# A fused attention and expert layer on one core: the expert weights' loads issued by SP from a row number in a register, with a new table of priorities

## What is computed

```python
xn = _layernorm(x, axis=-1)
x = x + _L0_attn_ref(xn, ...) + _L0_ffn_ref(xn, ...)
```

```python
topv, topi = jax.lax.top_k(gout, K)      # K = 2 of E = 8
z = (x @ W1 + b1) * (x @ W2 + b2)
g = z @ Wg + bg
y = (g * sigmoid(g) * (z @ Wl + bl)) @ W3 + b3
```

## Time and profile before

| what | value |
|---|---|
| median of 3 runs | 904.22 us (900.74 to 907.99) |
| the profiled execution, its own time | 901.63 us |
| its span | 899.9 us |
| PE busy | 662.3 us (74%) |
| DVE busy | 556.5 us (62%) |
| POOL busy | 508.1 us (56%) |
| ACT busy | 298.8 us (33%) |
| mean granted TensorE clock | 0.812 |

### The profile page before, as it was taken

The page is one execution under the profiler, slowest core; times in us unless marked ns, Lnnn a source line. Parts: engine busy times, 40 slices in busy tenths (PEclk is TensorE's granted clock), DMA queues, the critical chain, the costliest instruction groups (busy, mean ns, idle before and its releaser), DMA issues.

```text
span 899.9 us, 30793 instructions
## 1 busy us (share of the span) xinstructions
PE 662.3 (74%) x13276; PEld 506.4 (56%) x13276; DVE 556.5 (62%) x1233; ACT 298.8 (33%) x519; POOL 508.1 (56%) x565
## 2 busy tenths in 40 slices
PE   3345749788877896887796797778787887896741
PEld 2235737566656665665664565566565666674531
DVE  6899875548447747576538545774467665723651
ACT  2210043424335235243343343332434352313120
POOL 3722178848682864768724847756857654521311
PEclk9555569989789798888997898988969996878585
DMA  8212123232122131132221321422323302113341
GB/s 314 111 59 70 60 54 76 71 99 54 63 76 71 49 90 62 41 89 80 75 55 40 89 47 53 112 84 39 68 74 85 96 8 56 52 22 103 113 140 70
DMA packets 62950, 69.10 MB, mean 77 GB/s; under 512 B 40080, under 2 KB 45200, under 8 KB 62688
## 3 DMA queue, kind: packets, MB, share of 16 engines
q0 software_dynamic: 10672, 34.78, 13.6%
q1 hardware_dynamic: 51712, 30.42, 11.8%
q10 hardware_dynamic: 432, 1.94, 0.5%
HBM read 47.45 MB, written 19.66 MB: 75 GB/s over the span
## 4 chain that ended last, share of the span: by engine, by line
PE 27%; POOL 26%; issue 18%; DVE 17%; DMA 6%; ACT 4%; SPq 2%; POOLq 0%; DVEq 0%; ACTq 0%
POOL y_d L1034 6%; POOL xs L1009 4%; PE ps_shared L1614 4%; PE ps_g L1610 4%; POOL z L1068 3%; PE ps_x L1610 3%; DVE acc L1380 3%; POOL ssq_o L1060 3%; PE ps_shared L1752 2%; PE ps_l L1610 2%; PE ps_shared L1610 2%; DMA w_mid<-y_d 2%; POOL sumsq L974 2%; PE ps_shared L1619 1%; PE ps_shared L1668 1%
## 5 line engine op out<-in xcount | busy, mean ns | idle before, releaser
L1034 POOL DMA_INDIRECT y_d<-work,put_i x92 | 92.4, 1004 | 45.2 <-issue 26.5
L1009 POOL DMA_INDIRECT xs<-xn_d,owner_i x92 | 94.2, 1024 | 28.2 <-issue 26.3
L1610 PE MATMUL ps_g<-z,w_mid 128*128 128x512 f32 x276 | 87.7, 461 | 27.3 <-POOL z L1068 23.4
L1610 PE MATMUL ps_x<-xr,w_up 128*128 128x512 f32 x276 | 97.2, 468 | 12.3 <-issue 10.8
L1610 PEld LDWEIGHTS ps_g<-z,w_mid 128*128 128x128 f32 x276 | 58.1, 220 | 45.8 <-issue 33.4
L1380 DVE SCALAR_TENSOR_TENSOR acc<-pre,late_sb,acc 128x512 f32<-128x512 f32 x72 | 59.6, 828 | 39.0 <-ACT acc L1127 38.1
L1068 POOL TENSOR_TENSOR z<-work,z 128x512 fp32r<-128x512 f32 x46 | 59.8, 1299 | 39.1 <-ACT z L1234 38.7
L1610 PE MATMUL ps_l<-z,w_mid 128*128 128x512 f32 x276 | 79.1, 423 | 0.0
L1581 DVE SCALAR_TENSOR_TENSOR work<-ps_g,w_plain,work 128x512 f32<-128x512 f32 x46 | 34.3, 746 | 54.1 <-ACT work L1240 54.0
L1610 PEld LDWEIGHTS ps_x<-xr,w_up 128*128 128x128 f32 x276 | 53.7, 218 | 24.1 <-issue 11.5
L1240 ACT ACTIVATE work<-ps_g,w_plain 128x512 f32<-128x512 f32 x46 | 31.5, 685 | 103.0 <-PE ps_g L1610 103.0
(11 more groups left out here) (248 smaller groups left out, 1493.8 us busy)
## 6 DMA issues: line engine op xcount, KB each, us to landing
xa_d<-xr SPq DMA_DIRECT2D x8, 512.0 KB, 2.7
xa<-xa_d SPq DMA_DIRECT2D x8, 512.0 KB, 3.7
w_mid<-y_d SPq DMA_DIRECT2D x16, 256.0 KB, 3.4
system_d<-masked SPq DMA_DIRECT2D x8, 256.0 KB
x_res<-hidden SPq DMA_DIRECT2D x8, 256.0 KB, 2.8
part_d<-x_res SPq DMA_DIRECT2D x8, 256.0 KB
comb<-part_d SPq DMA_DIRECT2D x8, 256.0 KB, 2.8
out<-comb SPq DMA_DIRECT2D x8, 256.0 KB, 2.0
```

The source lines that it names most:

```text
L1009: pool.indirect_dma_start(xs[par][:, c, :], None, xn_d.rearrange("w p (c d) -> (w p c) d", c=CPW), bass.IndirectOffsetOnAxis(owner_i[:, w ...
L1034: pool.indirect_dma_start(y_d, bass.IndirectOffsetOnAxis(put_i[:, w * CPW + c:w * CPW + c + 1], 0), y_sb[par][:, c * D:(c + 1) * D], None) ...
L1610: made = pe.matmul(to, weights[a], x[b], start=start and n == 0, stop=stop and n == 2)
```

## The change

`load_split` and `load_plain` go from POOL's list to SP's. SP waits for the same semaphores as POOL did, reads the first row number of the tile from partition 0 of `row_i` into a register (`value_load`), and issues a plain transfer of 128 rows from there. The rows of one expert are neighbours in DRAM, so the same bytes are moved. The costs of the two steps in `FLOW` change with it, and the table of priorities `PULL` is a new one, with a second table `LEAN` beside it that was empty: a step's priority now also grows or falls with the number of its window or tile. Every engine's order is therefore another.

```diff
-    "load_split": [[(POOL_, 1.2, 7.0)]], "load_plain": [[(POOL_, 1.2, 5.0)]], ...
+    "load_split": [[(SP_, 1.2, 6.0)]], "load_plain": [[(SP_, 1.2, 4.0)]], ...
-PULL = {"beta_T": -100, "blend": 100, "choose": -200, "combine": -400, "conv": -150, "conv0": 150, "count": 300,
...
-LEAN = {}
+PULL = {"beta": -100, "blend": -50, "choose": 400, "conv": -350, "conv0": 450, "delta_T": 50, "delta_again": 400,
...
+LEAN = {"beta": -30, "beta_T": 15, "combine": 60, "delta_T": -35, "delta_again": -60, "down": 10.4, "fir": -5,
...
@@ block.sync @@
+                elif name == "load_split":
+                    sp.wait_ge(S["placed"], 1)
+                    if w:
+                        sp.wait_ge(S["up_low"], w)
+                        sp.wait_ge(S["mid_low"], w)
+                    row = sp.value_load(row_i[0:1, w:w + 1], min_val=0, max_val=(EXPERTS - 1) * P)
+                    sp.dma_start(w_split[:, :], expert_split[bass.ds(row, P), :]).then_inc(S["in_split"], 16)
+                elif name == "load_plain":
+                    if w < 2:
+                        sp.wait_ge(S["placed"], 1)
+                    else:
+                        sp.wait_ge(S["y_sb"], w - 1)
+                    row = sp.value_load(row_i[0:1, w:w + 1], min_val=0, max_val=(EXPERTS - 1) * P)
+                    sp.dma_start(w_plain[par][:, :], expert_plain[bass.ds(row, P), :]).then_inc(S[f"in_plain{par}"], 16)
@@ block.gpsimd @@
-                elif name == "load_split":
-                    pool.wait_ge(S["placed"], 1)
-                    if w:
-                        pool.wait_ge(S["up_low"], w)
-                        pool.wait_ge(S["mid_low"], w)
-                    pool.indirect_dma_start(w_split[:, :], None, expert_split,
-                                            bass.IndirectOffsetOnAxis(row_i[:, w:w + 1], 0)).then_inc(S["in_split"], 16)
-                elif name == "load_plain":
-                    if w < 2:
-                        pool.wait_ge(S["placed"], 1)
-                    else:
-                        pool.wait_ge(S["y_sb"], w - 1)
-                    pool.indirect_dma_start(w_plain[par][:, :], None, expert_plain,
-                                            bass.IndirectOffsetOnAxis(row_i[:, w:w + 1], 0)).then_inc(S[f"in_plain{par}"], 16)
```

More of the change, by code:

```diff
@@ L84 @@
     "choose": [[(DVE_, 5.0)], [(ACT_, 0.5)]], "count": [[(PE_, 1.2)]], "place": [[(DVE_, 9.0)]],
-    "load_split": [[(POOL_, 1.2, 7.0)]], "load_plain": [[(POOL_, 1.2, 5.0)]], "split_up": [[(ACT_, 0.65)], [(POOL_, 1.4)]], "split_mid": [[(ACT_, 1.1)], [(DVE_, 1.9)]],
+    "load_split": [[(SP_, 1.2, 6.0)]], "load_plain": [[(SP_, 1.2, 4.0)]], "split_up": [[(ACT_, 0.65)], [(POOL_, 1.4)]], "split_mid": [[(ACT_, 1.1)], [(DVE_, 1.9)]],
     "load_xs": [[(POOL_, 5.1, 7.6)]],
@@ L111 @@
 }
-PULL = {"beta_T": -100, "blend": 100, "choose": -200, "combine": -400, "conv": -150, "conv0": 150, "count": 300,
-        "delta_again": 350, "down": -300, "fetch": -100, "fir": 500, "fir_l": -400, "fir_l_T": -50, "fir_l_out": 150,
-        "fir_s_T": 200, "full": -100, "fuse": 300, "fuse2": 450, "gate_T": 50, "gates": 350, "gelu": 100, "hid": 100,
-        "inv": -400, "inverse_out": -50, "k_T": -50, "ln": -300, "load_plain": 200, "load_x": -50, "load_xs": -450,
-        "load_xt": 50, "masks": 350, "masks0": -600, "mid_g": 350, "mid_l": -250, "mix_s": -350, "mix_v": 300,
-        "norm": -300, "o": -200, "o_T_out": -100, "on_state": -250, "out": 600, "owned": 200, "place": 600, "q_T": -150,
-        "rank": -600, "rms": -350, "solve_mul": -500, "solve_sum": -100, "split": -50, "split_mid": 50,
-        "split_qkv": -50, "split_up": -50, "sumsq": -300, "swish": 500, "times": 300, "turn": 100, "u_adj": 500,
-        "up1": -300, "up2": 300, "v_T": 350, "v_act": -100, "v_again_T": -100, "v_b": -200, "w_T": -200, "w_T_out": 450,
-        "x_res": 300, "xn_out": 100, "y_out": -150, "z": 50, "zeros": -350}
@@ L122 @@
-LEAN = {}
+PULL = {"beta": -100, "blend": -50, "choose": 400, "conv": -350, "conv0": 450, "delta_T": 50, "delta_again": 400,
+        "diag": 150, "fir": -150, "fir_l": -600, "fir_l_T": 150, "fir_l_out": 150, "full": -100, "fuse": 250,
+        "fuse2": -50, "gate": -200, "gates": 500, "inv": 300, "inverse_out": -100, "ln": -50, "load_split": -400,
+        "load_x": -50, "load_xs": -600, "low": 300, "mark": 600, "masks": 250, "masks0": -300, "mid_g": 100,
+        "mid_l": -450, "mix_s": 250, "norm": -300, "normed": 50, "o": 600, "o_T_out": -150, "out": 50, "own": -100,
+        "owned": -150, "place": 500, "products": -200, "q_T": -150, "rank": -200, "rms": -350, "solve_sum": -100,
+        "split_mid": 450, "split_up": 200, "store": -400, "swish": 500, "turn": -50, "u_adj": -50, "up2": 600,
+        "v_T": -300, "v_again": -100, "v_again_T": 50, "v_b": -400, "w_T": 150, "w_T_out": 600, "x_res": -100,
+        "xn_out": -50, "y_out": 150, "y_put": -300, "z": -50, "zlow": -300}
@@ new lines @@
+LEAN = {"beta": -30, "beta_T": 15, "combine": 60, "delta_T": -35, "delta_again": -60, "down": 10.4, "fir": -5,
+        "fir_l_T": 30, "fir_l_out": -30, "full": 5, "fuse": -15, "fuse2": -5, "gate": 15, "gate_T": 5, "inv": -30,
+        "inverse_out": 10, "ln": -25, "load_split": -1.7, "load_xs": 5.2, "load_xt": -5, "mark": -30, "masks": 15,
+        "mid_l": 5.2, "mix_v": 30, "normed": 25, "o": -5, "o_T_out": -25, "owned": 30, "products": 30, "project": 5,
+        "rms": 10, "split": -1.3, "split_mid": 6.9, "split_up": -15.6, "state": 5, "store": 15, "sumsq": -15,
+        "times": 10.4, "u": 15, "u_out": 60, "v_T": 5, "v_act": 45, "v_again": -35, "v_again_T": -30, "v_b": -30,
+        "x_res": -5}
```

## The result

The changed kernel takes 909.77 us (median; 902.74 to 917.29), the kernel before 904.1 in the same series: ratio 1.0055, 95% interval 1.0032 to 1.0079. That is half a per cent slower, within the 1% that I had called no change; the forecast was 889 us. So of the 12.5 us between the two spans only 5.7 are the change's.

What follows compares the result with a forecast made beforehand. No engine was full; two interwoven streams of dependent steps bound the kernel, with POOL's time dearest. Terms -15 + 0 + 4 + 2 - 5 = -14 on the median 904.22 gave 890, stated as 889 us; range 868 to 913.

Steps and rivals of the forecast that it cites:

- POOL relief: Middle: 63 us leave POOL's list; at most 29 us come off the path, half taken, -15 us.
- the load's cost: Loads on SP: register read 1.2 us, landing 5 to 7 us as now, offset by less lateness; 0, ends at 5 us.
- SP in the way: SP's strict list: loads and the windows' system, solve and inverse steps queue behind each other; +4 us (0 to 30).
- start, from the loads: Start: three loads with register reads go out one after another, so DVE's `split_mid` waits; +2 us (0 to 3).
- the new order, tail: End: window 6's `fuse` products go ahead of the last `down`, removing waits for filter and gelu; -5 us (-10 to 0).
- Where I am least sure: All other instructions reordered: costs 0 if PE fills as well; one part in fifty per tile is 14 us either way.
- the whole of POOL's share comes off: POOL's full 29 us come off the path and the windows run earlier; 872 us, chance 0.17.
- the rival of SP as the knot: On SP, loads wait behind a solve or inverse not ready, and tiles wait for them; 928 us, chance 0.12.
- The one queue: On SP's queue, a solve or inverse read right behind a load waits for all of it; 904 us, chance 0.08.
- The signs that I had named: Right: POOL busy about 458 us, chain share near 22%; wrong: ACT's `w_split` waits over 60 us, PE's middle share not above 80%.

Runs made afterwards that it cites:

- series 5: Chip where the kernel before takes 905.73 us: old order with loads on SP 880.14 us (0.9710); changed kernel with both tables emptied 911.21 us (1.0075).
- series 2: Against the kernel before (996.74 us): changed kernel 0.9842; old order with loads on SP 0.9607; old order with nearly all weight loads left out 0.9576.
- series 3: Old order, loads on SP, POOL keeping the old loads' waits 0.9716, time 0.9673, both 0.9765; changed kernel with later `y_put` 0.9875; all against the kernel before.
- series 4: Old order, loads on SP, POOL's waits kept, plus spare transfers: large indirect 1.0014, small indirect 1.0047, plain 0.9772; changed kernel with `LEAN` emptied 1.0161.

## Why the prediction was wrong

The sum of the prediction, beside what the two traces of the 905 us kind and the old order with loads on SP give:

| term | forecast, us | measured, us | from |
|---|---|---|---|
| POOL relief, the load's cost, SP in the way (the middle) | -15 + 0 + 4 = -11 | -23.7 | 658.3 to 634.6 |
| start, from the loads | +2 | +0.6 | 151.8 to 152.4 |
| the new order, start | 0 | +3.7 | 152.4 to 156.1 |
| the new order, middle | 0, "14 us either direction" | +43.4 | 634.6 to 678.0 |
| the new order, tail | -5 | -13.0 | 91.3 to 78.3 |

The loads alone moved the tail by +1.5 (89.8 to 91.3). The old order with loads on SP was profiled in series 5, the other two before any series, so that a few us of each row can be the chip's. And the executions are not equally typical: that of the changed kernel lies 4.1 us above its median, that of before 2.5 below, that of the old order at it. So the order's rows sum to some 4 us too much. By the ratios, the same is 0.971 for the loads and 1.0055 / 0.971 = 1.036 for the order: about -26 and +32 us.

**The step that failed** is the one under "Where I am least sure": that an order of all other instructions "that fills it as well as now costs 0", with 14 us either way. It cost +34 us between the spans, +32 by the ratios. I had priced the moves that I looked at, the four loads at the start, window 3's inverse and the last tile, and let the rest cancel; nothing in the trace of before spoke for that, and a range of one part in fifty was too narrow for a list that is new from end to end. That 909.77 still lies inside my range of 8 in 10 (868 to 913) is luck: two misses of opposite sign met, the loads -26 where I had -9 and the order +32 where I had -5. What can be said of these 34.1 us: 12.2 are PE's busy time (655.8 to 668.0, at a granted clock of 0.86 instead of 0.89 in the middle), 21.9 its idle time. Between the cuts PE's busy time grows by 21.2; 9.9 of it is attention's work of the last stretch (46.23 to 36.29), which moved there. The tail's gain is in part only a move, and the middle pays for it. The idle time that nothing in the profile explains, summed over the groups of PE and PEld, is 270.7 us in the old order with loads on SP and 320.1 in the changed kernel (in PE's own rows, where no gap counts twice, 42.7 and 70.7). So the added idle time is of the kind that the profile puts down to no other engine. Why the new order has more of it, and which of its many swaps does it, no run told apart. The empty tables' 1.0075 suggests that the new tables as a whole hold no good order for these costs, rather than that one entry spoils it.

**The POOL relief** had the right sign and was too small. Taking half of 29 us was wrong for the size; the upper end, POOL's share of the chain (46%) times the 63 us that left it, was near what the loads alone gave (-26 us between medians). The rival "the whole of POOL's share comes off" forecast 872 for the sum with the tail's -5; without the order's part it would be 877, measured 880.14. Whether that nearness is the mechanism or luck stays open. The same rule fails on the slower chips. The kernel before, profiled again in series 2, has these busy times and this chain:

```profile
PE 718.2 (72%) x13276; PEld 538.3 (54%) x13276; DVE 563.3 (57%) x1233; ACT 299.6 (30%) x519; POOL 506.4 (51%) x565
...
PE 41%; issue 18%; DVE 15%; POOL 11%; DMA 6%; ACT 4%; another core or an unknown queue 2%; SPq 2%; DVEq 0%; POOLq 0%; ACTq 0%
```

By the rule, POOL's 11% of 996.8 us is 22% of its busy time, and 22% of 63 us is 14 us. The loads alone gave 39 there (996.74 to 958.1). What POOL's time and waits were worth in series 3, 1.3% or 13 us, fits the 14; the rest came off with the indirect transfers themselves, a cost that my sum did not have at all. On the first kind of chip the gain was not taken apart.

**The load's cost on SP.** From the start of the register read to the issue 0.7 us pass, where I had 1.2 for the read; the read's own record is 0.27 us long, under my lower bound of 0.3. The landing takes 4.4 us where I had 5 to 7. The Trainium skill ("DMA: Bandwidth & Descriptors", "Latency and other measured facts") gives a floor of about 600 ns for a `tensor_load`; the two groups of reads have medians of 270 and 272 ns and 467 at most, so the records of the reads lie below it, and the measurement decides; the 0.7 us up to the issue lie above it. The term 0 held: no loads at all is within 0.3% of loads on SP, with overlapping intervals, so that SP's loads add no cost that these runs can tell.

**SP in the way**, and the rival of SP as the knot, fell: ACT's waits for `w_split` stay at 46.3 us, under the 60 that I had set, SP waits for the buffer at 16 of the 23 loads, and the new order is dear with the loads on POOL too (1.0334). **The one queue** fell with it: by the rule of the Trainium skill ("DMA: Bandwidth & Descriptors", "Queues, rings and completion order") a solve read behind a load waits for it. 10.7 MB more in SP's queue moved the ratio from 0.9716 to 0.9772, in two series whose intervals overlap, so no run here shows a wait of weight. DVE's waits for solve reads did rise, from 17.3 us before to 30.1 in the changed kernel. But they are 19.0 in the old order with loads on SP, and on the slower chips 25.7 in the changed kernel and 24.0 in the new order with the loads on POOL: they go with the order, not with the loads in SP's queue.

**The end** was right in kind and too small in size (-5 forecast, -11.5 measured, in part a move): no wait between the last `down` and `fuse2`, forecast under 2 us, and 13.9 us between them shrank to none (809.4 to 823.25).

**The signs that I had named** misled in part. POOL's 458 came (461.0), its share of the chain fell even more, to 13%, and no sign of failure from ACT appeared; all of them speak of the loads, which did work. The one that speaks of the order, PE's share in the middle not rising above 80 of 100, did appear over the whole middle: 533.5 of 658.3 (81.0%) before, 545.8 of 678.0 (80.5%) after, and 82.7% in the old order with loads on SP. In the single stretch of the earlier trace rows it rose, from 80.1 to 81.2: a hundred us is too short to read it.

## What to carry to other kernels

When a change comes with a new order, run the old order with the mechanical edit alone first: here that version gains 3 to 4% and beats both kernels, and the replanned order threw it away. Price a wholly new order with a range as wide as the largest term of the rest, not with 0. And don't trust the share that an engine has on the chain, times what leaves it, as an estimate: it gave 29 us where 26 were measured, and 14 where 39 were, since it prices the engine's own time and not what the transfers do to others.

## What the hardware showed that I had not expected

- The same kernel takes 904 to 906 us in two series and 990 to 1,003 on four other chips. Between the trace of before and that of series 2 the spans differ by 96.9 us. DVE's busy time differs by 6.8, ACT's and POOL's by under 2; PE's busy time grows by 55.9 (662.3 to 718.2) and its idle time by the rest, 41.0. The granted clock is no explanation by itself: executions of 990.38 us at 0.827 and of 910.67 us at 0.802 are both on record. One group shows both parts. The filters' 32x32 products take 229 ns each in the row of series 4 and 228 on the first chip, but they overlap less (47.6 us busy there, 35.0 here), and the idle time in front of them that nothing explains is 30.6 us there and 8.0 here (the kernel before, first chip):

```profile
L1773 PE MATMUL ps_shared<-head_vs,taps 32*32 32x32 f32 x2048 | 35.0, 228 | 8.8 <-issue 8.0 <-DVE xr L1278 0.8
```

- On the slower chip of series 4 an indirect transfer issued by POOL costs about 0.6 us (27 us for 46), with 8 KB as with 201 or 262 KB, and PE's unexplained idle time grows with it. In the kernel before of series 2, 50% of the time of PE's unexplained gaps (those under 3 us, in the middle) lies inside an indirect transfer of POOL, which is 28% of the time. On the first chip it is 32% of the gaps in 31% of the time: no such link. There the loads' new way gains 2.9% all the same, and the same sum of unexplained idle time falls by 15 us only (286.0 to 270.7; in PE's own rows not at all, 42.4 to 42.7), so that more of the gain there may lie in POOL's own time and waits; it was not taken apart on such a chip, and stays open. How an indirect transfer holds PE up is open too.
- The changed kernel is 1.6% faster than before on a slower chip and 0.6% slower on a faster one, as the loads' way gains a little more there (3.4 to 3.9% against 2.9) and the new order costs a little less (2.4 to 3.3% against 3.6). Of the order's costs, the 3.3 is with the loads on POOL, and the 3.6 is put together from two series. A ratio between two such kernels is a property of the chip as well.
